# Cross attention of a decoder layer: in odd steps the next batch's projection piece stands ahead of the turn of the probabilities

## The reference

```
xn = layer_norm(x) ; cn = layer_norm(context)          # 32 x 112 x 256 and 32 x 375 x 256
q = xn @ Wq ; k, v = split(cn @ Wkv)                   # 16 heads of 64 columns
sim = (q * 64**-0.5) @ k.T                             # 112 x 375 for each head
attn = softmax(where(mask, sim, -max))
out = (attn @ v).reshape(b, n, 1024) @ Wo              # then x = norm(x + out)
```

## Time and profile before

| what | us |
|---|---|
| runs: median of 3 (lowest to highest) | 2285.5 (2284.28 to 2299.6) |
| the profiled execution, its own time | 2295.51 |
| its span, first to last instruction | 2293.8 |
| busy TensorE matmul / weight load | 2203.9 / 1648.7 |
| busy VectorE / ScalarE / POOL | 1530.7 / 1384.9 / 761.7 |

### The profile page before, as it was taken

The page is one execution under the profiler, slowest core; times in us unless marked ns, Lnnn a source line. Parts: engine busy times, 40 slices in busy tenths (PEclk is TensorE's granted clock), DMA queues, the critical chain, the costliest instruction groups (busy, mean ns, idle before and its releaser), DMA issues. The chain is left out here.

```text
span 2293.8 us, 57837 instructions
## 1 busy us (share of the span) xinstructions
PE 2203.9 (96%) x20778; PEld 1648.7 (72%) x20778; DVE 1530.7 (67%) x4396; ACT 1384.9 (60%) x3178; POOL 761.7 (33%) x1335
## 2 busy tenths in 40 slices
PE   5999999999998999999999999999999999989997
PEld 3776866867867667777777777777777777868886
DVE  4555455446447677777777777777777777465657
ACT  4556356356355476767676767676767676544534
POOL 1121122112115244444444444444444444200003
PEclk8999999999999999999999999999999999789999
DMA  5100000000001100000000000000000000043202
GB/s 138 41 2 1 0 0 0 0 0 0 15 19 38 41 10 16 10 16 10 16 10 16 10 16 10 16 10 15 11 15 11 15 4 2 1 112 109 75 1 65
DMA packets 45732, 51.44 MB, mean 22 GB/s; under 512 B 19120, under 2 KB 37664, under 8 KB 45504
## 3 DMA queue, kind: packets, MB, share of 16 engines
q1 hardware_dynamic: 45504, 48.45, 7.1%
HBM read 44.78 MB, written 3.67 MB: 21 GB/s over the span
## 5 line engine op out<-in xcount | busy, mean ns | idle before, releaser
L1723 POOL TENSOR_SCALAR arena<-arena,p_rec 112x375 f32<-112x375 f32 x512 | 303.0, 593 | 633.0 <-DVE p_rec L1589 633.0
L64 PE MATMUL b_pb<-arena 128*125 128x512 f16 (+1 forms) x1364 | 380.0, 299 | 1.5 <-DVE k_lo L1560 1.5
L66 PE MATMUL b_pb<-arena 128*125 128x512 f16 (+1 forms) x1364 | 377.9, 298 | 0.0
L65 PE MATMUL b_pb<-arena 128*125 128x512 f16 (+1 forms) x1364 | 377.3, 297 | 0.0
L1593 DVE TENSOR_TENSOR pt_lo<-b_t,pt_hi 125x336 f16<-125x336 f32 x512 | 258.0, 504 | 166.6 <-ACT pt_hi L1484 165.4
L1575 DVE CUSTOM_DVE_ANT_0 arena<-b_s,arena 112x375 f32<-112x375 f32 x512 | 274.8, 537 | 99.4 <-PE b_s L1338 89.0
L1484 ACT ACTIVATE pt_hi<-b_t 125x336 f16<-125x336 f32 x512 | 227.1, 444 | 139.7 <-PE b_t L1347 137.7
L1478 ACT ACTIVATE arena<-arena,neg_max 112x375 f32<-112x375 f32 x512 | 308.0, 602 | 1.4 <-DVE neg_max L1575 1.4
L1347 PE MATMUL b_t<-ident,arena 112*125 112x112 f32 x1536 | 275.5, 289 | 8.8 <-POOL arena L1723 2.6
L1347 PEld LDWEIGHTS b_t<-ident,arena 112*125 112x125 f32 x1536 | 216.6, 191 | 50.0 <-POOL arena L1723 26.9
L952 POOL TENSOR_SCALAR_AFFINE_SELECT sm<-sm 112x448 f32<-112x448 f32 x128 | 71.8, 583 | 422.4 <-ACT sm L632 422.4
(11 more groups left out here) (279 smaller groups left out, 5762.0 us busy)
## 6 DMA issues: line engine op xcount, KB each, us to landing
arena<-in_L_ffn_W_dram SPq DMA_DIRECT2D x16, 1024.0 KB, 7.4
arena<-in_ctx_dram SPq DMA_DIRECT2D x32, 375.0 KB
out_dram<-c_z SPq DMA_DIRECT2D x8, 448.0 KB, 3.2
x_sb<-in_x_dram SPq DMA_DIRECT2D x1, 3136.0 KB, 19.0
ff<-in_L_attn_w_dram SPq DMA_DIRECT2D x2, 1024.0 KB, 6.3
ff<-in_L_xattn_Wkv_dram SPq DMA_DIRECT2D x2, 1024.0 KB, 5.3
arena<-in_mask_BxS_bf_dram SPq DMA_DIRECT2D x32, 41.0 KB, 2.6
a_raw<-in_L_attn_wq_dram SPq DMA_DIRECT2D x1, 1024.0 KB, 5.1
```

Source lines behind the costliest of these rows:

```text
L64: pe.matmul(out, lh, rh, start=first, stop=False)
L65: pe.matmul(out, lh, rl, start=False, stop=False)
L66: return pe.matmul(out, ll, rh, start=False, stop=last)
L1723: pool.tensor_scalar(p32[:, h % 4, :], p32[:, h % 4, :], p_rec[:, h % 4:h % 4 + 1], 0.0, ALU.mult, ALU.add).then_inc(p_norm_done, 1)
```

## The change

In odd steps, in all batches but the last, `piece` comes ahead of `turn_scores` on TensorE, and `piece_high` ahead of `turned_high` on ScalarE. Even steps and the last batch stay as they are. The orders of VectorE, POOL and the DMA queue are not touched, nor is any instruction, tile or semaphore.

```diff
@@ TensorE, body(b, par) @@
                 for s in range(H):
+                    if s % 2 == 1 and not is_last(b):
+                        piece(b + 1, 1 - par, s)
                     turn_scores(b, s)
-                    if not is_last(b):
+                    if s % 2 == 0 and not is_last(b):
                         piece(b + 1, 1 - par, s)
-                    else:
+                    if is_last(b):
                         if s > 0:
                             route_logits(s - 1)
                         route_turn(s)
@@ ScalarE, body(b, par) @@
                         softmax_exp(b, s + 2)
                     elif not is_last(b):
                         softmax_exp(b + 1, s + 2 - H)
+                    if s % 2 == 1 and not is_last(b):
+                        piece_high(b + 1, 1 - par, s)
                     turned_high(b, s)
-                    if not is_last(b):
+                    if s % 2 == 0 and not is_last(b):
                         piece_high(b + 1, 1 - par, s)
-                    else:
+                    if is_last(b):
                         route_columns(s)
```

## The result

| what | before | changed |
|---|---|---|
| first comparison, median (lowest to highest) | 2285.41 (2284.28 to 2299.6), 4 runs | 2328.57 (2321.4 to 2331.66), 4 runs |
| ratio, 95% interval | | 1.0164 [1.0132, 1.0196] |
| second comparison (run e5 below) | 2297.94 (2290.05 to 2306.59), 11 runs | 2319.54 (2315.12 to 2325.54), 6 runs |
| ratio, 95% interval | | 1.0089 [1.0065, 1.0114] |
| profiled execution, span | 2293.8 | 2323.9 |

The change makes the kernel slower, by 1.6% in the first comparison and by 0.9% in the second. I had forecast 2311.5 us, 26 us or 1.1% more, in a range of 2291 to 2332. Between the two profiled executions, on which the sum was made, the difference is 30.1 us.

What follows compares the result with a forecast made beforehand. TensorE bounds the kernel, its scores held by the path from the odd turn to the maximum; +0.78 us per batch over 31 batches is 24.2, plus 1.5, so +26 us: 2311.5 us, range 2291 to 2332.

Steps and rivals of the forecast that it cites:

- What bounds the kernel: Cross-attention: TensorE sets the time; its even-step scores wait on the path from the odd turn through `pt_hi`, `pt_lo`, reciprocal, maximum.
- The path's terms: End of odd piece to next scores, through ScalarE's high part, `pt_hi`, `pt_lo`, reciprocal, maximum: 2.23 us for k, 2.35 for v.
- The exposed load of the piece: TensorE, odd steps: the piece's first weight load behind the values exposes 0.04 us, bounds 0 and 0.11.
- The estimate of 0.02: TensorE, k and q pieces: loads of 128 columns use a fast path and expose 0.02 us, loss about 3 us smaller.
- Two turns in a row at 0.31 each: TensorE, each pair of steps: the odd and even turns, now adjacent, cost 0.31 us each.
- 0.31 for every turn: Sign to look for on TensorE in the changed kernel: each turn lasts 0.31 us; behind the values it lasted 0.42.
- Step 7 at nothing: Odd step with piece v2: head 8's turn waits for POOL whatever the order, scores stay at 3.78 us: 0 change.
- Batch 30: Prepares nothing, so steps 9 and 11 have no context turn beside the path: 1.5 us added to the sum.
- The last batch at no cost: Only 31 batches carry pieces; in the last one the diff changes nothing.
- Median and profile: Profiled execution lies 10 us above the runs' median 2285.5; carried over unchanged, so 2321.5 profiled becomes 2311.5 us.

Runs made afterwards that it cites:

- e5: The changed kernel again, no edit, beside the kernel before: 2319.54 us, ratio 1.0089 [1.0065, 1.0114].
- e3: Changed kernel, with VectorE's odd steps doing reciprocal and masked maximum ahead of the low part of the turned probabilities: 2276.39 us, ratio 0.9927.
- e1: Kernel before with only the TensorE half of the change, ScalarE keeping its old order: 2302.5 us, ratio 1.0043.
- e2: Kernel before with only the ScalarE half of the change, TensorE keeping turn ahead of piece: 2406.53 us, ratio 1.0478.
- e6: Changed kernel with POOL's preparation later (reciprocal roots behind head 8's normalisation), VectorE untouched: 2322.95 us, ratio 1.0105.
- e4: Kernel before with VectorE's odd steps doing reciprocal and masked maximum ahead of the low part, TensorE and ScalarE unchanged: 2291.19 us, ratio 0.9967.

## Why the prediction was right, and where it was off

- **What bounds the kernel.** Right. e3 shows it most plainly: the path cut, and the loss turns into a gain.
- **The path's terms.** Right to 0.01 us for the k piece, 2.24 against 2.23. Each term but the read-out's 0.08 us was a measured distance between starts, not a duration: the high part lasts 0.49 us but the next instruction of ScalarE starts 0.38 us behind it. With its duration that link alone would have come out 0.1 us long in each pair. e1 and e2 changed the first two terms, and the batch came out at 38.50 for 38.5 and 41.59 for 41.8.
- **The exposed load of the piece.** Right in kind, off in size. I took 0.04 us from an fp16 product with 112 weight columns. In the changed kernel the first two matmuls of a k piece start 0.17 us apart, later ones 0.16: 0.01 exposed. For the v piece with its 125 columns it is 0.05 (starts at 1416.53, 1417.23 and 1417.88, three matmuls apart: 0.70, then 0.65). The estimate of 0.02 that I drew from the Trainium skill (TensorE: Matmul & The Clock Gate, section on the weight-path perf modes) for the 128-column loads was nearer than the row, and the trace agrees with that section in that less is exposed with 128 columns than with 125 (0.01 against 0.05). Six steps at 0.04 were 0.24 us of the 0.78 per batch, and about 0.1 was right. The total came nearer than that, 0.73 us per batch from the rows above against 0.78, because small misses of a few hundredths went the other way, the q piece's step above all (7.07 for 7.04, next bullet). That part is luck.
- **Two turns in a row at 0.31 each.** Right: six transposes, then the next piece, 1401.66 to 1402.31, take 0.65. But my sign "0.31 for every turn" did not hold: the turn of head 3, which now stands between the q piece and the output projection, takes 0.37 (1406.27 to 1406.64), and that of head 10 takes 0.39 (1423.10 to 1423.49).
- **Step 7 at nothing.** Right, and e6 shows the reason: both waits end within a tenth of a microsecond of each other. The normalisation of head 8 ends at 1418.45 us, 1.92 behind the values, to the hundredth as before.
- **Batch 30.** I had it at 0.78 + 1.5 = 2.3 us; from its first scores to the first of the last batch it takes 38.74 in place of 36.22, 2.5 us more. The size is right, the reason only in part. The distances from step 8 to 12 were 4.20 and 4.26 without context turns, and the path makes 4.38 and 4.87 of them: that is 0.8 us. As much comes from step 14 to the last batch's step 0, where 3.45 becomes 4.38: before, neither a turn of x nor, in step 0, a piece stood ahead of those scores, and now they wait 1.04 us for the maximum. I had not counted that. With 29 batches at 0.74 and batch 0, which is 0.2 shorter, this makes 23.8 of the 23.9 us. My sum for these batches was 25.7.
- **The last batch at no cost.** In the two profiles this term is off: "in the last one the diff changes nothing", but it took 5.3 us longer at a lower granted clock. 23.9 + 5.3 and 0.9 elsewhere are the 30.1 us. The single runs below give no sign that the change causes this.
- **Median and profile.** I carried the 10 us between the profiled execution of before and its median over, as if they belonged to the kernel. They don't, and this is why 2311.5 us lies 17 us under the first median and 8 under the second. Three of the first four runs of before lay near 2285 us, while its medians in the later sets are 2295 to 2300. That is why the first ratio is 1.0164 and the second 1.0089; that my 1.1% lies between them is in part luck.

**Runs of equal clock.** Nearly every run has its span and its mean granted clock on record, and together they tell the change from the scatter. Over its 41 runs with a clock on record, the kernel before goes from 2280.6 us at 0.988 to 2312.2 us at 0.975, some 2 us for each 0.001; the three early runs near 2285 us have no clock on record, but all later runs of before under 2285 us had 0.987 or 0.988. At 0.979 the span of before is 2296.6 to 2300.5 us (9 runs) and that of the changed kernel 2323.7 to 2323.9 (3 runs): 25 us or 1.1% between the middles, beside 23.9 us counted in the batches and 26 forecast. In the same way e4, which its interval does not tell from before, lies 8 to 10 us under it: 2290.3 to 2290.8 against 2298.5 and 2300.8 at 0.978, 2270.5 and 2271.6 against 2280.6 and 2281.7 at 0.988. Its batches are 0.26 us shorter, 8 us in all.

The scatter lies in large part in the last batch. In e1 that batch has the same instructions in the same orders as in the changed kernel, and its five distances between scores are 4.85, 6.89, 5.25, 4.85 and 5.27 us; in the changed kernel they are 4.85, 11.71, 5.25, 8.30 and 8.30. Windows of steps 6 to 8 there, e1 and changed:

```profile
1987.75:1992.60 4.85, 4.54 (x56) 3.84 (x55) 2.34 (x11) 3.05 (x8) 1.95 (x4) 1.00 0.00 0
```
```profile
2005.96:2014.26 8.30, 8.29 (x55) 6.97 (x55) 2.51 (x12) 3.05 (x8) 2.54 (x5) 0.50 0.00 0
```

The same work takes 4.85 us at a granted clock of 1.00 (2.4 GHz) and 8.30 at 0.50 (1.2 GHz). From its first scores to its last turn the batch takes 37.7 us in e1, whose whole run had 0.988, and 55.4 in the changed kernel, whose run had 0.979. Up to its step 2 the two profiles show the same, TensorE busy 4.54 of 4.85 us at 1.00 and 0.99; behind it the changed kernel's profile has 0.57 in steps 2 to 4.

What stays open is why the clock falls there in one run and not in another, and whether the change has a small share in it. The mean clock of the changed kernel over its 10 runs is 0.981, as is that of before over its 41, which leaves room for a few microseconds either way and shows nothing regular.

## What to carry to other kernels

Before an instruction is moved in a hand-written order, list for each engine what stands behind the moved instruction's consumers in that engine's order, and which of those the busiest engine needs next; the loss here came three instructions behind the wait that the change made longer. An engine with 40% idle time can still cost 5% if it takes work in the wrong order. And when two waits end within a tenth of a microsecond of each other, removing one wins only their difference until the other is gone too, so edits are to be tried in pairs before they are given up. Where the scatter comes from the granted clock, compare runs of equal clock.

## What the runs showed that I had not expected

- What the first matmul behind the values costs more than a later one depends on the form: for three fp32 transposes 0.1 us (0.42 against 0.31), for an fp16 piece with 125 weight columns 0.05, for one with 128 columns 0.01.
- A kernel whose cross-attention batches nearly all repeat to within 0.02 us still scatters by more than 1% from run to run, and the profiles put most of it into some 60 us in which TensorE has the router's small products among its work and the granted clock falls to 0.65 or 0.71 in the mean. A gain of 8 to 10 us elsewhere is hidden by it in the medians (e4) and comes out between runs of equal clock.
- POOL's power instruction for the reciprocal roots of four numbers per partition takes 1.04 us, more than the normalisation of a whole row of 375 at 0.59, and stood ahead of it.
